# First attention's rows weighed in their own group's turn, in a function of its own

## What is computed

```python
scores = jnp.sum(Q[col] * (K[row] + rel), axis=-1) / np.sqrt(DK)    # one per edge and head
m = segment_max(scores, col)
e = jnp.exp(scores - m[col])
attn = e / segment_sum(e, col)[col]
out = segment_sum(attn[:, :, None] * V[row], col)
```

## Time and profile before

| what | before |
|---|---|
| median of 3 runs | 3595.72 us (3586.8 to 3599.15) |
| the profiled execution's own time | 3572.16 us |
| its span in the trace | 3570.5 us |
| mean granted PE clock | 0.908 |
| PE, DVE, ACT, POOL busy | 81%, 46%, 30%, 31% of the span |
| first attention's reductions, first to last start | 294.2 to 925.9 us |

### The profile page before, as it was taken

The page is one execution under the profiler, slowest core; times in us unless marked ns, Lnnn a source line. Parts: engine busy times, 40 slices in busy tenths (PEclk is TensorE's granted clock), DMA queues, the critical chain, the costliest instruction groups (busy, mean ns, idle before and its releaser), DMA issues. The chain is left out here.

```text
span 3570.5 us, 54651 instructions
## 1 busy us (share of the span) xinstructions
PE 2906.6 (81%) x17789; PEld 2076.3 (58%) x17789; DVE 1630.6 (46%) x2730; ACT 1058.1 (30%) x2952; POOL 1118.4 (31%) x1072
## 2 busy tenths in 40 slices
PE   5405888888864687888884999999999977999997
PEld 4404777777653576777772555555555544555554
DVE  7825777777741466666645213141414143030302
ACT  0001444444331355555542112130404042010102
POOL 5555666666315455555523001010101002020200
PEclk9857999999876799998985999999999988999998
DMA  6237888888233377666743533324242404333331
GB/s 232 75 114 216 263 256 255 256 257 254 93 122 79 73 119 126 118 117 114 123 70 109 175 113 108 124 85 135 85 131 69 134 0 159 113 102 119 100 120 36
DMA packets 330861, 477.67 MB, mean 134 GB/s; under 512 B 148534, under 2 KB 241414, under 8 KB 329940
## 3 DMA queue, kind: packets, MB, share of 16 engines
q1 hardware_dynamic: 271492, 297.49, 29.8%
q0 software_dynamic: 59088, 176.67, 17.5%
HBM read 417.29 MB, written 58.52 MB: 133 GB/s over the span
## 5 line engine op out<-in xcount | busy, mean ns | idle before, releaser
L862 PE MATMUL e_part_ps<-e_onehot,e_from_src 128*128 128x129 f32 x3328 | 572.2, 295 | 115.6 <-issue 68.5
L966 ACT ACTIVATE sums<-e_part_ps 128x384 f32 x832 | 412.5, 496 | 599.2 <-PE e_part_ps L864 302.9
L862 PEld LDWEIGHTS e_part_ps<-e_onehot,e_from_src 128*128 128x128 f32 x3328 | 463.1, 196 | 182.5 <-issue 104.8
L2111 PE MATMUL gin_sum_ps<-slab,high 128*128 128x391 f16 x2000 | 498.2, 331 | 2.2 <-DMA slab<-adj 1.6
L2111 PE MATMUL gin_sum_ps<-slab,low 128*128 128x391 f16 x2000 | 497.7, 331 | 0.0
L674 POOL DMA_INDIRECT e_from_src<-val,src x416 | 394.1, 947 | 308.7 <-PE e_part_ps L864 137.3
L674 POOL DMA_INDIRECT e_from_src<-vk,src x416 | 394.2, 948 | 277.6 <-PE e_part_ps L864 146.8
L864 PE MATMUL e_part_ps<-e_onehot,e_small 128*65 128x129 f32 x1664 | 327.4, 279 | 6.8 <-issue 6.7
L1805 PE MATMUL sage_sum_ps<-slab,high 128*128 128x391 f16 x1200 | 300.3, 332 | 11.6 <-DVE z_t L1928 6.4
L742 DVE TENSOR_TENSOR e_from_src<-e_from_src,e_fixed 128x2048 f32<-128x2048 f32 x104 | 237.5, 2284 | 136.5 <-ACT e_fixed L947 100.2
L1805 PE MATMUL sage_sum_ps<-slab,low 128*128 128x391 f16 x1200 | 299.6, 331 | 0.0
(11 more groups left out here) (286 smaller groups left out, 4306.7 us busy)
## 6 DMA issues: line engine op xcount, KB each, us to landing
slab<-adj SPq DMA_DIRECT2D x160, 977.5 KB, 4.8
e_window<-q_part SPq DMA_DIRECT2D x416, 128.0 KB
adj<-e_counts SPq DMA_DIRECT2D x8, 1250.0 KB
adj<-e_counts SPq DMA_DIRECT2D x8, 1193.8 KB
e_from_src<-vk,src POOLq DMA_INDIRECT x416
e_from_src<-val,src POOLq DMA_INDIRECT x416
e_window<-alpha_part SPq DMA_DIRECT2D x416, 4.0 KB
vk<-pr_out SPq DMA_DIRECT2D x25, 256.0 KB, 2.0
```

The lines of the kernel that those rows point to most:

```text
L862: nc.tensor.matmul(part_ps[s][:, k * ENDS:(k + 1) * ENDS], from_src[:, b, j, k * P:(k + 1) * P], onehot[:, b, j, :], start=True, stop=True)
L966: nc.scalar.activation(keep["sums"][:, :, bass.ds(starts[j], P)], of[:, :, 0:P], ACT.Copy).then_inc(whole_copied, 1)
L2111: mm = nc.tensor.matmul(sum_ps[KH * n + m][:, 0:AN], part[:, t, m * P:(m + 1) * P], slab[:, s, n, k * AN:(k + 1) * AN], start=(t == 0 and ...
```

## The change

A new function `attend_rows` has its own order of the work, and the first attention calls it; the second goes on calling `attend_edges`, which is unchanged. The operations of first attention, their sizes and their buffers are the same. DVE weighs group g in turn g, between match 2 and match 3. PE sums all 8 chunks of group g-1 in turn g, in pairs. It spreads chunks 0, 1 of group g+2 at the end of turn g, and chunks 2, 3 of group g+1 at its start. ACT copies sums 0 to 3 before the exponential and 4 to 7 behind it, with the copy of the turned slots between copies 5 and 6. The loops over turns go through a helper that calls `tick` in order and leaves out what does not exist at either end. SP's and POOL's queues are written as before.

```diff
@@ the turn of each engine in attend_rows, first attention's parts (+), beside attend_edges' (-)
 # DVE
-                take_scores(g)
-                match(g + 1, 0)
-                weigh_rows(g - 1)
-                scan_peaks(g)
-                match(g + 1, 1)
-                spot_slots(g + 2)
-                match(g + 1, 2)
-                shift_scores(g)
-                match(g + 1, 3)
+                    nc.vector.tensor_reduce(score[:, r, :].rearrange("p (j h) -> p j h", h=H),
...
+                if layer == 0 and after:
+                    match(*after, 0)
+                v.wait_ge(t_turned, g + 1)
...
+                if layer == 0 and after:
+                    match(*after, 1)
+                if later:
+                    spot_slots(*later)
+                v.wait_ge(chunk_summed[(b - 2) % RING], G * it + (G if b >= 2 else 0) + 1)
+                v.wait_ge(t_back, g + 1)
...
+                if layer == 0 and after:
+                    match(*after, 2)
+                v.wait_ge(prob, g + 1)
+                nc.vector.tensor_tensor(
+                    from_src[:, b, :, 0:D].rearrange("p j (h d) -> p j h d", h=H),
+                    from_src[:, b, :, 0:D].rearrange("p j (h d) -> p j h d", h=H),
+                    share(r).unsqueeze(3).to_broadcast([P, G, H, DK]), ALU.mult).then_inc(weighted, 1)
+                if layer == 0 and after:
+                    match(*after, 3)
 # PE
-                sum_parts(g - 2, (4, 5))
-                spread_windows(g + 1, (0, 1))
-                turn_scores(g)
-                spread_windows(g + 1, (2, 3))
-                sum_parts(g - 2, (6,))
-                spread_windows(g + 1, (4, 5))
-                sum_parts(g - 2, (7,))
-                sum_parts(g - 1, (0,))
-                turn_peaks(g)
-                sum_parts(g - 1, (1,))
-                spread_windows(g + 1, (6, 7))
-                sum_parts(g - 1, (2,))
-                turn_slots(g + 2)
-                sum_parts(g - 1, (3,))
+                if layer == 0 and after:
+                    spread_windows(*after, (2, 3))
+                if before:
+                    sum_parts(*before, range(0, 2))
+                turn_scores(*group)
+                if before:
+                    sum_parts(*before, range(2, 4))
+                if layer == 0 and after:
+                    spread_windows(*after, (4, 5))
+                turn_peaks(*group)
+                if before:
+                    sum_parts(*before, range(4, 6))
+                if later:
+                    turn_slots(*later)
+                if layer == 0 and after:
+                    spread_windows(*after, (6, 7))
+                if before:
+                    sum_parts(*before, range(6, G))
+                if layer == 0 and later:
+                    spread_windows(*later, (0, 1))
 # ACT
-                copy_sums(g - 2, range(4, G))
-                copy_sums(g - 1, (0, 1, 2))
-                copy_turned(g + 2)
-                weigh(g)
-                copy_sums(g - 1, (3,))
+                if before:
+                    copy_sums(*before, range(0, 4))
+                weigh(*group)
+                if before:
+                    copy_sums(*before, range(4, 6))
+                if later:
+                    copy_turned(*later)
+                if before:
+                    copy_sums(*before, range(6, G))
@@ the helper, and the call
+        def ticks(eng, tick):
+            def at(it, b, first, last):
+                before = (it, b - 1) if b else None if first else (it - 1, RING - 1)
+                after = (it, b + 1) if b + 1 < RING else None if last else (it + 1, 0)
+                later = (it, b + 2) if b + 2 < RING else None if last else (it + 1, b + 2 - RING)
+                tick(before, (it, b), after, later)
...
-                attend_edges(nc, keep, 0, scratch["vk"], scratch["q_part"], 2 * D, D, float(DK) ** -0.5)
+                attend_rows(nc, keep, 0, scratch["vk"], scratch["q_part"], 2 * D, D, float(DK) ** -0.5)
```

318 lines of the change are left out of this document (added).

## The result

| | before | after |
|---|---|---|
| median of 20 runs each | 3590.81 us (3584.0 to 3599.15) | 3600.62 us (3594.37 to 3610.55) |
| ratio | | 1.0029, 95% interval 1.0021 to 1.0037 |
| span of the profiled execution | 3570.5 us | 3602.4 us |
| first attention's reductions, 51 turns | 631.7 us, 12.39 a turn | 659.5 us, 12.93 a turn |

The forecast was 3569 us, 0.75% faster. The change made the kernel 10 us slower, 0.29%: inside the range, on the other side of no change, and at the edge of what I had called measurable. It lies in the band that the prediction called unchanged, 3585 to 3607 us, to which it gave 0.18.

What follows compares the result with a forecast made beforehand. A ring of hand-overs, 12.35 us a turn, was taken as the bound. New ring: 7.3 + 0.35 + 1.70 + 1.03 + 0.10 + 0.95 = 11.4, with 0.4 idle 11.8; 49 turns save 27 us: 3595.7 - 27 = 3569, range 3540 to 3624.

Steps and rivals of the forecast that it cites:

- the band that the prediction called unchanged: Whole kernel: 3585 to 3607 us, chance 0.18, if PE is fuller than drawn or another ring takes over.
- Then hand-over 1.70: New ring: wait from the slots' end on PE to ACT's copy, taken as 1.70 us, the old mean.
- rival one: First attention: late PE signals count twice in the new ring; 12.8 us a turn, 22 us slower, 3618; chance 0.32.
- the sum: First attention: new ring added up from PE work, bank wait, hand-over, copy and first spread, 11.4 us a turn.
- the ring: First attention: hand-overs from one first spread through the slots and ACT's copy to the next, 12.35 us before.
- 0.4 kept for idle: First attention: of PE's idle before its sums, 0.9 us a turn, 0.4 was kept in the new turn.
- The forecast's 11.8: First attention: predicted turn of 11.8 us against 12.35 before, saving 27 us over 49 turns.
- At 1.2 it adds 0.35: New ring: sum 3 needs sum 0's bank; with signals 1.2 us late this adds 0.35 us a turn.
- of nearly one lateness: DVE before the first scan: a wait for turned scores of nearly one signal lateness, 1.2 to 1.7 us.
- sum 3 starting a whole lateness later: Rival one's chain on PE: with lateness L, sum 3 starts at 2.35 + L instead of 3.2 us.
- Rival two: First attention: PE really works until its late signals, so order is worth nothing, 3596 us; within the 0.18 for unchanged.
- PE's own work as 10.7 us a turn: First attention: PE's busy time, 10.7 us a turn, as floor; at most 81 us saved.

Runs made afterwards that it cites:

- copy_first: Changed kernel with ACT's copy of the turned slots ahead of the copies of sums 4 and 5; 3610.31 us, 1.0096 of the kernel before.
- early_slots: Changed kernel with slots spotted before the scans, turned before the peaks, copied before the exponential; 3586.25 us, 1.0030 of the kernel before.
- half_sums: Kernel before and changed kernel, features 128 to 255 of V not summed in first attention; 3585.56 and 3595.53 us, 1.0030 and 1.0059 of the kernel before.
- sp_rows_2: Kernel before, with plain DMAs of neighbouring rows from SP's queue in place of POOL's gathers after the first round; 3610.29 us, 1.0044.
- no_gather: Kernel before and changed kernel, first attention gathering only its first 4 groups; 3460.11 and 3458.04 us, 0.9690 and 0.9685 of the kernel before.

## Why the prediction was wrong

**The step that failed.** "Then hand-over 1.70": I carried the old mean into a new queue. I had written that the copies of sums 4 and 5 stand in front of the slots' copy, but in rival one and not in the sum. They are two copies in a row, 1.17 us, that ACT can begin only when sum 4's late signal is in (592.53, where the sum is recorded as ending at 590.00 in the same timeline), about when the slots' signal would be in too. Measured 2.75 and 2.74 us against 1.70; copy_first, which takes only those copies out of the way, gives 1.69; and without gathers the orders are 0.91 apart at this place. The rest of the ring came out as summed: 8.90 and 8.83 us from first spread to the slots' end, where the sum has 0.95 + 7.65 and 0.4 kept for idle, 9.0. The forecast's 11.8 plus 1.05 is 12.85, and the reductions between 400 and 850 us stand 12.81 us apart. In the sum one term carries the miss. That a ring without the two copies would take 11.8 us is not shown: copy_first and early_slots left such copies between the slots and the first spread.

**A second, smaller miss.** "At 1.2 it adds 0.35", and a wait "of nearly one lateness" before the scan, about 1. The turned scores came 1.5 us late in the mean (2.0 in the turn shown), DVE idled 2.33 us there, and PE waited 0.5 us a turn for the peaks, where my sum has none. The sum has the bank of sum 0, which sum 3 needs, but not that of sum 4, which sum 7 needs: PE waited for it in 30 of the 35 turns, 0.3 us in the mean. My sum has 0.35 us for sum 3, a wait that did not come, and 0.4 kept for idle without a source, 0.75 in all. That the waits which did come are about as long is luck. And the sum has nothing for the clock. It fell from 1.00 to 0.97 between 400 and 850 us, and at the full clock the orders are 0.3 us a turn apart, not 0.5.

**Right.** The end of the first spread to the slots' end was 7.65 us by the sum and is 7.86 in the turn shown. The slots' copy still releases the first spread, after 0.10 us. DVE's wait before the matches went from 2.9 to 0.7 us, and a new one stands before the first scan. No DMA became the limit. The rest of the kernel moved little: span less stage is 2938.8 and 2942.2 us before, 2942.9 and 2948.0 after.

**Rival one came out by its signs, and half by its mechanism.** 12.8 us turns, idle above 2 us before the scan and hand-overs above 1.9 are what it listed, and it had the copies of sums 4 and 5 in front of the slots. Its other half, sum 3 starting a whole lateness later, did not show: PE had no idle in front of sum 3 in the mean. Its price, 22 us, was too high against the medians' 10 and 12; it is nearer to the profiles' stages, 17 to 28 us apart, and part of the 28 is the clock.

**Rival two fell** with half_sums, and with sp_rows_2 and no_gather, whose signals are on time. The rule of the Trainium skill (Perfetto Trace Analysis, Tensor Engine Instruction), that a matmul's end is estimated and its signal waits for PSUM, explains how records and signals can differ; here it was no sign of work.

**PE's floor.** I took PE's own work as 10.7 us a turn from its busy time, and as the limit of any gain. It is 9.93. In turns with waits more busy time is recorded for the same matmuls, in sp_rows_2 too (375.95 us in 35.5 turns, 10.6, with signals on time); whether they are drawn longer or ran slower is not shown. So some 2.4 us a turn, 120 us over the stage, come with the gathers, and no order tried here wins any of them.

**Open.** Whether taking ACT's copies out of the ring altogether would gain is untested. It would need an order in which neither the slots' copy nor that of sum 4 is still standing in ACT's queue when the first spread is due. At half the gathers the old order is 0.9 us a turn better, at all of them only 0.3 to 0.5. A candidate is the loop from a chunk's summing to the next gather into its slot, which holds late signals in both orders; that is only argued. A gather of two chunks in one instruction, which would halve their number, wasn't tried. No kernel run here with all of the work beat the kernel before.

## What to carry to other kernels

Price a chain by its hand-overs as well as its work: for each signal that crosses engines, ask how late such signals run in this trace, and what stands ahead of the receiving instruction in its in-order queue, for all of that may be worked off after the late signals are in. Before reordering against a wait, take away some work of the engine that looks bound and look whether the time moves; here half of the sums left out gained nothing, while leaving out the gathers gained 114 us. Read the granted clock beside such a test, for it went from 1.00 to 0.95 and 0.92 and may have taken part of what there was to gain. When you move an instruction out of a chain, follow what it now stands in front of: copy_first freed the slots' copy and held up a bank that the same first spread waits for, one sum further on.

## What the chip showed that I had not expected

While GpSimd issues a gather about every 1.25 us, the slots are noticed 1.7 us after their recorded end in the mean, and up to 3.5 us has been seen at a match; without gathers, or with plain DMAs of the same traffic from SP's queue, 0.13 us. Bytes matter little to the turn: at 164 GB/s it is 12.9 us, at 257 it is 12.4. And it may depend on the chip: one ran the same kernel in 3267 us where the other jobs took 3574 to 3597, with a profiled edit of it at 9.97 us a turn under as many gathers. What differs stays open. A change of this size must therefore be compared on one chip, and may be worth something else on another.
